# Pool stage of a four-layer graph kernel: the scatter of overflow maxima issued behind the next group's first gathers

## What is computed

```python
h = relu(layernorm(x)); x = x + L0(h, adj)    # o = relu(adj @ (h @ W0) + b0); max over each row's neighbours of o
h = relu(layernorm(x)); x = x + L1(h, adj)    # concat(h, adj @ h) @ w1
h = relu(layernorm(x)); x = x + L2(h, adj)    # hyperbolic layer, two products with adj
h = relu(layernorm(x)); x = x + L3(h, adj)    # graph layer, four nearest neighbours by distance, second product
```

## Time and profile before

| | |
|---|---|
| median of 3 runs | 1799.66 us (1797.57 to 1802.69) |
| the profiled execution, its own time | 1797.79 us |
| its span in the profile | 1796.1 us |
| busy shares of the span | PE 88%, DVE 70%, ACT 40%, POOL 33% |
| scatters L1374, eight | first at 411.4 us, last at 745.1 us |
| L1763 `take_block` | 240 times, 683 ns each |
| L1342 gathers | 160 times, 1049 ns each |
| L1374 scatter | 8 times, 1033 ns |

### The profile page before, as it was taken

The page is one execution under the profiler, slowest core; times in us unless marked ns, Lnnn a source line. Parts: engine busy times, 40 slices in busy tenths (PEclk is TensorE's granted clock), DMA queues, the critical chain, the costliest instruction groups (busy, mean ns, idle before and its releaser), DMA issues.

```text
span 1796.1 us, 32841 instructions
## 1 busy us (share of the span) xinstructions
PE 1587.6 (88%) x9151; PEld 928.5 (52%) x9161; DVE 1261.5 (70%) x3487; ACT 724.0 (40%) x1143; POOL 587.3 (33%) x817
## 2 busy tenths in 40 slices
PE   4999999867777778799997999999999999859987
PEld 4777777522333333456664666778544444324544
DVE  7899999856677677646555666642699999933434
ACT  3444444334455555213333222666555555500000
POOL 5333333356655556401110000233000000165663
PEclk8999999977898888899999999999999999978998
DMA  7687787422222222132222222444000000033442
GB/s 246 222 307 283 291 297 288 152 59 70 69 74 73 68 75 75 43 106 93 93 82 83 82 93 87 118 133 124 31 0 6 12 6 6 12 100 126 141 129 72
DMA packets 127159, 198.70 MB, mean 111 GB/s; under 512 B 11859, under 2 KB 96889, under 8 KB 118912
## 3 DMA queue, kind: packets, MB, share of 16 engines
q1 hardware_dynamic: 102592, 172.58, 27.9%
q0 software_dynamic: 11840, 19.18, 3.8%
q10 hardware_dynamic: 12672, 6.29, 1.2%
HBM read 178.13 MB, written 26.21 MB: 114 GB/s over the span
## 4 chain that ended last, share of the span: by engine, by line
PE 66%; DVE 14%; issue 12%; ACT 3%; another core or an unknown queue 3%; DMA 1%; POOL 1%; ACTq 0%; DVEq 0%; POOLq 0%; SPq 0%
PE bank L681 27%; PE bank L606 8%; PE bank L567 7%; PE bank L751 6%; DVE partsA L2149 5%; PE bank L595 4%; PE bank L818 3%; DVE cand L1623 3%; PE bank L530 2%; PE bank L572 2%; PE bank L543 2%; ACT first L919 2%; PE bank L520 1%; PE bank L819 1%
## 5 line engine op out<-in xcount | busy, mean ns | idle before, releaser
L681 PE MATMUL bank<-partsB,panel 128*128 128x387 bf16 (+1 forms) x2048 | 367.2, 338 | 46.2 <-issue 32.7
L681 PEld LDWEIGHTS bank<-partsB,panel 128*128 128x128 fp8e4 x2048 | 204.6, 100 | 204.4 <-issue 65.9
L818 PE MATMUL bank<-wide,partsA 128*128 128x512 f32 x512 | 263.3, 596 | 6.9 <-ACT rows L1138 4.9
L606 PE MATMUL bank<-first,partsB 128*128 128x512 fp8e4 x768 | 238.9, 426 | 5.3 <-issue 5.3
L919 ACT ACTIVATE first<-bank 128x512 fp8e4<-128x512 f32 x256 | 150.4, 597 | 210.1 <-PE bank L595 91.5
L1763 DVE TENSOR_TENSOR gath<-gath,bank 128x512 f32<-128x512 f32 x240 | 162.9, 683 | 102.1 <-PE bank L606 59.7
L1623 DVE MAX8 cand<-bank 128x8 f32<-128x128 f32 x1024 | 216.9, 286 | 10.4 <-PE bank L572 7.8
L567 PE MATMUL bank<-partsA,panel 128*128 128x387 bf16 x1024 | 212.3, 329 | 7.5 <-DVE cand L1623 6.3
L1342 POOL DMA_INDIRECT gath<-pool_features,idx_now x160 | 167.9, 1049 | 84.6 <-issue 57.9
L595 PE MATMUL bank<-panel,tri 128*128 128x512 fp8e4 x256 | 109.5, 430 | 94.5 <-ACT first L919 67.2
L873 ACT ACTIVATE panel<-bank 128x1024 fp8e4<-128x1024 bf16 x128 | 130.9, 1024 | 147.8 <-PE bank L543 147.8
(11 more groups left out here) (298 smaller groups left out, 2159.4 us busy)
## 6 DMA issues: line engine op xcount, KB each, us to landing
rows<-in_adj SPq DMA_DIRECT2D x64, 1024.0 KB, 7.0
panel<-adjT_panels SPq DMA_DIRECT2D x96, 512.0 KB
panel<-adjT_panels SPq DMA_DIRECT2D x128, 256.0 KB
adjT_panels<-panel SPq DMA_DIRECT2D x32, 512.0 KB, 3.0
gath<-pool_features,idx_now POOLq DMA_INDIRECT x160
overflow_maxima<-wide POOLq DMA_DIRECT2D x1, 2048.0 KB, 18.3
pool_features<-gsc ACTq DMA_DIRECT2D x8, 256.0 KB, 2.3
rows<-overflow_maxima SPq DMA_DIRECT2D x8, 256.0 KB
```

Source lines behind the costliest of these rows:

```text
L606: i = pe.matmul(pool_bank[j % 4][:, :], pparts[:, j, k * FE:k * FE + F], first_slot[:, j % SLOTS, :], start=(k == 0), stop=(k == 2))
L681: i = pe.matmul(bank[q][:, 0:3 * w], panel[:, q, j, :], of_block if w < FE else parts_of[u][:, j, :], start=(j == 0), stop=(j == NT - 1))
L818: pe.matmul(o[:, :], zs[:, q % 2, :], zT[:, c * 512:(c + 1) * 512], start=True, stop=False)
```

## The change

On GpSimd the scatter of group `g` moves from behind the gathers of tile 3 of group `g` to behind the gathers of tile 0 of group `g+1`. The last group's stands after the loop. The first turn of the loop is now written out on its own (`turns`), since it has no scatter. On VectorE two joins and what follows move by two to four blocks: L1820 and L1823 from behind blocks 7 and 8 to behind 9 and 10, and each later step to match. No instruction of TensorE, ScalarE or SyncE moves, and no arithmetic is added or taken away.

```diff
--- before.py
+++ after.py
@@ -1377,13 +1377,13 @@
             def turn(g, peeled):
                 for q in range(G):
                     gathers(g, q)
+                    if q == 0 and not peeled:
+                        store_overflow(g - 1)
                     if q == 1:
                         rows_landed(g, q)
                         overflow_gathers(g)
-                    if q == 3:
-                        store_overflow(g)
-            with pool.Fori(0, NG) as g:
-                turn(g, False)
+            turns(pool, turn)
+            store_overflow(NG - 1)
             pool.wait_ge(s_parts, 3 * NG)
             with pool.Fori(0, NG) as g:
                 split(3, g)
@@ -1875,15 +1875,17 @@
                     if not peeled:
                         if 3 <= j < 6:
                             tree(before, G - 1, j - 3, (g, G - 1))
-                        if 6 <= j < 9:
-                            pool_floor(before, j - 6)
+                        if j == 6:
+                            pool_floor(before, 0)
                         if 9 <= j < 11:
-                            pool_post(before, j - 9)
-                        if 14 <= j < 16:
-                            pool_post(before, j - 12)
-                        if j == 16:
+                            pool_floor(before, j - 8)
+                        if j in (12, 14):
+                            pool_post(before, j // 2 - 6)
+                        if 15 <= j < 17:
+                            pool_post(before, j - 13)
+                        if j == 20:
                             pool_post(before, 5)
-                        if j == 20:
+                        if j == 21:
                             pool_post(before, 4)
                         if j == 30:
                             operand(1, g - 1)
```

## The result

The changed kernel took 1815.33 us (median of 4, 1809.69 to 1824.61), the kernel before 1798.62 us (median of 4, 1796.27 to 1802.69). The ratio is **1.0098, 95% interval 1.0072 to 1.0124**: slower, by more than the 0.3% bound, and by more than the forecast 1808. The profiled execution of after took 1824.61 us, the longest of its four, and that of before 1797.79. Of the 26.8 us between them 24 lie in the Pool stage: the last L1763 ends at 773.6 us, before at 749.4.

The account below looks back on a forecast made before the run. The prediction took TensorE's chain in the Pool stage as the bound, its results seen late in long gather runs. Six periods at +1.7 us gave +10 us on 1797.8, so 1808 us, range 1785 to 1822; joins and peeled turn counted nothing.

Parts of the forecast that it names:

- What bounds the kernel: Pool stage: TensorE's chain bounds, GpSimd's gathers and scatter are not in it; TensorE's results are seen late in long runs.
- Step 1: New period's start: scatter 1.34 us, then tile 1, landing and index copy 8.91 us; 10.25 us, 7.3 blocks.
- the waits at L1374: GpSimd's scatter waiting for VectorE: about 9 us each after the change, where there were 4 to 5.
- Step 2: Long run of overflow gathers and tile 2: 5 blocks in 4.8 us, then 4 in 10.55 us.
- Step 4: Tile 0's gathers in tile 3's run: 6.5 us at 2.3 to 2.64 us a block, 2.8 to 2.5 blocks.
- Step 5: Pause until the scatter's release: 8 blocks left at 1.15 us each, 9.1 to 9.4 us.
- The sum: Pool stage period 47.8 to 48.1 us against 46.3; +1.7 taken, six times, makes +10 us.
- The joins at nothing: VectorE's later joins (L1820 and neighbours) put at no cost; at most 7 us in all if tight.
- tile 0's gathers wait for ScalarE's clear: Rival at tile 0's gathers: a held block breaks the run and the delay; about no effect, no chance of its own.
- GpSimd was the bound after all: Rival in the Pool stage: faster, full price 27 us (1770), milder form 1783 to 1791; chance 0.24.

Follow-up runs that it names:

- experiment 3: Changed kernel plus a GpSimd wait for tile 3's landing ahead of the next tile 0's gathers: 1803.18 us, 1.0014 of the kernel before.
- experiment 4: Kernel before plus a GpSimd wait for the landing of tile 2's first gather, breaking the long run: 1792.47 us, ratio 0.9958.
- experiment 1: Only GpSimd's part of the change (scatter moved), VectorE's joins as in the kernel before: 1816.45 us against 1799.71, ratio 1.0085.
- experiment 2: Only VectorE's part of the change (later joins), GpSimd's order as in the kernel before: 1800.29 us, ratio 1.0011.
- experiment 5: Kernel before with three GpSimd memsets between tile 2's first gather and the other four, on the second chip: 1732.75 us against 1720.95, ratio 1.0074.
- experiment 6: Kernel before with the short lists' 160 indirect gathers as direct DMAs of fixed rows, on the second chip: 1629.99 us against 1720.95, ratio 0.9469.
- experiment 10: Kernel before with three GpSimd memsets after tile 2's first gather, repeated on the third chip: 1731.79 us, ratio 1.0058.
- experiment 11: Kernel before with the short lists' 160 indirect gathers as direct DMAs of fixed rows, repeated on the third chip: 1628.95 us, ratio 0.9463.

## Why the prediction was right, and where it was off

- **What bounds the kernel**: right on the first chip. It is TensorE's chain, held by late results in long runs; experiments 3 and 4 show that breaking a run pays. That this is true of one chip only was not in the prediction, and no row of a single trace could say it.
- **Step 1 and the waits at L1374**: the scatter, tile 1 and its landing 10.9 us (567.6 to 578.5), predicted 10.25. Waits of about 9 us were predicted. The seven are 4.2 to 12.4 us, 8.2 on the mean. At three of six borders the ten indirect DMAs in a row are there, with a granted clock below 1.00 and idle readers, as described.
- **Step 2, long run**: predicted 5 + 4 blocks in 15.35 us. In 526.1 to 542.1 it was 2.62 + 2.26 us of busy time, 7 blocks in 16.0. Two blocks are missing, and at the pause's 1.25 us each they are 2.5 us. Over the whole stage too the runs are slower than the windows of before let me expect: 1.40 us a block in their first 4.8 us, against 1.16. **This is the term that was mis-sized**: rates of stretches were carried over to a new order as if they belonged to the stretch. By what is issued, it is the overflow gathers that hold 34 and 38 blocks in 62.5 and 62.7 us (after, experiment 1), where before had 44 in 63.1; tile 2's five, where the delay was seen first, are as before (11 and 13 in 44, before 11). By the place in a run, it is in experiment 1 the next 3.2 us that are slow (3.2 us a block, 2.0 in before) and the first are not, so where exactly it falls isn't settled, nor why.
- **Step 4, tile 0's stretch**: predicted 2.3 to 2.64 us a block; 3.3 and 1.9 in two groups. Over the three unbroken runs it is 8 blocks in 19.3 us, 2.4 each, over all six borders 20 in 37.9 (1.9), and in experiment 1 16 in 37.4 (2.3). The mean is right; a single group is not.
- **Step 5, the pause**: 1.15 us a block predicted, 1.25 over all pauses of the stage.
- **The sum**: +10 us was forecast, +20.1 recorded. The six periods with a border grew by 17.3 us, 2.9 each and not 1.7: 7.1 us more than forecast. The seventh grew by 2.8 us, where the forecast had nothing; it has no run of ten and five gathers fewer than before, so the length of a run may not be all of it; in experiment 1 it grew by 0.4 us only. The profiled execution is itself 9 us over its median; by the medians the change cost 16.7 us, and by experiment 1's periods (351.0 against 333.7) 17.3. The direction was forecast from the right mechanism; the size was 1.7 to 2 times the forecast, and that the time lies in the range owes something to the range's width.
- **The joins at nothing**: right (experiment 2), and after has no wait at L1820 on the first chip.
- **The rival "tile 0's gathers wait for ScalarE's clear"** came true in part: at three of six borders (2 to 3, 5 to 6, 6 to 7) GpSimd stood 2.8, 2.8 and 0.9 us between tile 3's and tile 0's gathers. The profile says "issue", but each time ScalarE's clear L948 ends 0.9 us before tile 0's first gather (at 502.5, 657.5 and 704.1 us), and at the first two of these borders another L948 had ended 0.9 to 1.0 us before tile 3's. The rival said that the loss goes with it. It didn't: those three periods grew by 2.3, 2.3 and 4.2 us, the unbroken ones by -0.7, 7.2 and 2.1. In experiment 1 two borders were broken, and grew by 3.2 and 2.6 us; the four unbroken ones by 0.1, 2.1, 2.8 and 6.1. Why a broken run costs as much was not separated.
- **The rival "GpSimd was the bound after all"** is what two other chips show; the change itself was timed on one of them, and gained 0.39% in place of the rival's 1.5%. There the scatter's wait that was to go did not exist (0.30 us of idle time); what the move bought was tile 0's earlier gathers, and the new wait at L1820 took part of it.

**What stays open.** Why TensorE's results come late on one chip and not on two others, with the same program. Each of the other two was met in one set of runs only, so the chip itself and whatever else differed at that time are not told apart. Whether the results are late or only the word of them: the rows of TensorE can't tell. Why experiment 3 is so much faster than the change with almost as many late results. Whether a pause helps because nothing is issued in it or because the gathers land. Whether on the first chip direct DMAs or a pause filled with computing would end the delay: experiments 5, 6, 10 and 11 were meant to tell, and all met chips without it. So "indirect DMAs hold the signals back" is shown as to place and length of the runs, by experiments 1 and 4 (by experiment 3 in the time only), and not as to the kind of DMA. Whether the joins moved two blocks further would win more on the faster chips wasn't tried.

## What to carry to other kernels

A wait that stands in the profile is not a price until the chain passes through it; here the 4.8 us in which GpSimd idled were time in which TensorE and VectorE went at 1.15 us a block, and not at 2 or more, and a wait added elsewhere made the kernel faster. Look at what an engine's neighbours do while it is busy without a gap, by counting units of progress (a taken block) in windows, not only at what it waits for. And before a change of one per cent is kept or dropped, time it on more than one chip: the same edit was +0.98% on one and -0.39% on another, because another engine was the bound. Of the versions timed that leave nothing out, the kernel before with the wait in its long run was the best where it takes 1800 us (0.9958), and the change where it takes 1721 (0.9961); none was shown to be best on both.

## What the runs showed of the hardware that was not expected

- **One program took 4.5% longer on one chip than on two others**: 1798.62 us (1796.27 to 1802.69) against 1720.95 (1717.61 to 1722.31) and 1721.28. The profiled executions on the first and the third are 79 us apart. The Pool stage makes 37 of it (the last L1763 ends at 749.4 and 712.7 us), and the gathers of the last stage another 37: they ran from 1578.8 to 1778.7 us on the first and from 1544.9 to 1708.2 on the third, 200 against 163 us. Some 9 us more lie behind the last gather. Between the two stages they agree within 3 us. First the windows of before on the first chip, then on the third (PE, PEld, DVE, ACT, POOL busy (x), PEclk, DMA, GB/s); the last row of each is a part of the last stage.

```profile
30.00:358.00 328.00, 307.82 (x3133) 227.65 (x3133) 305.23 (x1319) 148.62 (x165) 114.78 (x337) 0.96 0.70 258
358.00:718.00 360.00, 268.57 (x1150) 118.00 (x1150) 244.13 (x528) 175.13 (x303) 214.69 (x211) 0.84 0.24 70
...
760.00:1540.00 780.00, 757.36 (x3586) 444.74 (x3593) 544.79 (x1277) 357.70 (x599) 85.28 (x58) 1.00 0.20 66
1540.00:1710.00 170.00, 139.09 (x693) 72.94 (x693) 84.03 (x143) 20.78 (x38) 91.21 (x98) 0.87 0.32 102
```

```profile
30.00:358.00 328.00, 306.63 (x3134) 227.39 (x3133) 306.51 (x1323) 148.94 (x168) 114.89 (x339) 0.97 0.71 257
358.00:718.00 360.00, 281.27 (x1253) 117.98 (x1254) 263.25 (x578) 186.33 (x323) 232.39 (x229) 0.92 0.27 75
...
760.00:1540.00 780.00, 754.80 (x3512) 438.49 (x3510) 565.04 (x1264) 374.47 (x630) 89.74 (x62) 0.99 0.20 63
1540.00:1710.00 170.00, 160.27 (x958) 93.52 (x955) 79.59 (x188) 0.98 (x2) 127.94 (x138) 0.98 0.48 148
```

 Both slow stages are those in which GpSimd issues indirect DMAs in long runs, and there the granted clock is 0.84 and 0.87 against 0.92 and 0.98. The last stage's 128 gathers are one unbroken run on the third chip; on the first it is broken into sixteen, the longest of 28.
- **A matmul's recorded end says little of when others may read it.** A result was seen up to 14.5 us after it on one chip (experiment 3; 12.5 us in the kernel before), never more than 0.21 us on two others. (The Trainium skill, "Perfetto Trace Analysis", section "Tensor Engine Instruction (MATMUL, LD_WEIGHTS)", says that the end is an estimate and the semaphore comes after the PSUM write. The traces agree as far as they go: TensorE's rows look alike on both chips, 0.38 us for an L595 and 0.81 us for three of L606, also where the reader came 4.9 us late.)
- **A direct DMA is cheaper to issue than an indirect one**: five in 2.77 us (experiment 11, one row of GpSimd), where five indirect ones of the same size take 6.5 us. On GpSimd's timeline of experiment 11:

```profile
517.86 1.05 POOL L1345 DMA_INDIRECT gath<-pool_features,rest  x1 [0.30 <-issue]
518.91 2.77 POOL L1342 DMA_DIRECT2D gath<-pool_features  x5
```

 With that the whole kernel takes 5.4% less on a chip on which GpSimd bounds the stage, as it does with one indirect gather a tile; both leave out part of the maxima. (By the Trainium skill, "DMA: Bandwidth & Descriptors", section "Rules for kernel authors", a DMA is to be issued early and waited for late; the change does so with tile 0's gathers. Where the kernel before took 1721 us the runs agree, by 0.39%; where it took 1799 they do not, by 0.98%.)
